# Edge payload in another space, a join that doesn't wait for it, and twenty chunks of own rows gathered in the sort phase

## The reference, cut to what matters

```python
# layer 0: softmax aggregation over the edges of a node, then an MLP 32 -> 64 -> 32
msg   = relu(h[src]) + 1e-7
alpha = segment_softmax(msg * beta, dst)
out   = mlp(segment_sum(msg * alpha, dst) + h)
# layer 1: an MLP on [h_dst, h_src - h_dst] of each edge, with two batch norms
# layer 2: two spline convolutions over the 3 attributes of an edge
# layer 3: three convolutions (GINE) over the 8 attributes of an edge
```

## Time and profile before

| | us |
|---|---|
| median of 3 timed runs | 6416.72 |
| their range | 6408.68 to 6420.33 |
| span of the profiled execution | 7419.8 |
| VectorE busy, GpSimd busy | 4474.0, 4471.1 |
| end of the sort phase in the profile | about 1349 |
| end of layer 0 in the profile | about 1995 |

### The profile page before, as it was taken

One profiled execution on the slowest core, in us unless ns is written; L12 is line 12 of the kernel. 1 busy time (PEld: TensorE's weight loads), 2 busy tenths in 40 slices (PEclk: granted clock), 3 DMA queues, 4 the chain that ended last, 5 costly groups with the idle time before them and its releaser, 6 DMA issues. The chain is left out here.

```text
span 7419.8 us, 40111 instructions
## 1 busy us (share of the span) xinstructions
PE 2391.5 (32%) x7897; PEld 1532.4 (21%) x7897; DVE 4474.0 (60%) x8498; ACT 1488.7 (20%) x2709; POOL 4471.1 (60%) x4334
## 2 busy tenths in 40 slices
PE   0000000001422220003556577623336665666222
PEld 0000000000311110001334355422223332333111
DVE  8745978896278583545888567646645554555111
ACT  0000000120201120101212122234424443444000
POOL 7777571577367527755553466467756646563666
PEclk9999999998655565555666677755568887887555
DMA  1111110111277511312322122255534433443111
GB/s 41 30 37 16 34 26 4 24 23 22 61 100 112 81 44 40 79 51 58 71 67 60 31 53 53 43 76 90 93 54 70 70 64 58 69 70 65 41 43 36
DMA packets 646154, 400.37 MB, mean 54 GB/s; under 512 B 357903, under 2 KB 603572, under 8 KB 645671
## 3 DMA queue, kind: packets, MB, share of 16 engines
q0 software_dynamic: 138304, 79.39, 14.4%
q1 hardware_dynamic: 488316, 291.24, 13.7%
q10 hardware_dynamic: 19306, 27.35, 1.1%
HBM read 221.09 MB, written 179.22 MB: 54 GB/s over the span
## 5 line engine op out<-in xcount | busy, mean ns | idle before, releaser
L969 POOL DMA_INDIRECT gin_ring<-tab,QB x784 | 790.0, 1008 | 482.2 <-DVEq L2642 241.4
L969 POOL DMA_INDIRECT c_ring<-tab,QB x784 | 775.7, 989 | 432.0 <-issue 223.5
L1747 PE MATMUL c_psU<-spline,c_hzT 97*128 97x288 f32 x1568 | 633.6, 561 | 218.4 <-DVE c_V L1702 188.5
L969 POOL DMA_INDIRECT c_ring<-a_tab,b_place x392 | 383.7, 979 | 345.1 <-DMA x_lin<-c_ring 151.2
L1509 POOL DMA_INDIRECT nodes<-H,a_out x392 | 435.5, 1111 | 192.4 <-issue 127.0
L969 POOL DMA_INDIRECT l_ring<-in_x_dram,a_own x376 | 429.3, 1142 | 188.8 <-issue 114.3
L969 POOL DMA_INDIRECT sort_ring<-xe_tab,b_place x392 | 422.7, 1078 | 171.1 <-issue 118.9
L2692 POOL DMA_INDIRECT out_dram<-out_rowr,out_idxr x392 | 385.9, 984 | 203.4 <-issue 121.8
L969 POOL DMA_INDIRECT l_ring<-agg_tab,QA x392 | 404.6, 1032 | 156.3 <-issue 125.7
L969 POOL DMA_INDIRECT sort_ring<-in_x_dram,sort_raw x392 | 413.0, 1054 | 120.3 <-issue 119.2
L1747 PEld LDWEIGHTS c_psU<-spline,c_hzT 97*128 97x128 f32 x1568 | 390.8, 266 | 381.3 <-issue 259.7
(11 more groups left out here) (643 smaller groups left out, 7541.7 us busy)
## 6 DMA issues: line engine op xcount, KB each, us to landing
tab<-c_rows SPq DMA_DIRECT2D x147, 128.0 KB
a_tab<-l1s_rows SPq DMA_DIRECT2D x49, 304.0 KB
x_lin<-c_ring SPq DMA_DIRECT2D x49, 256.0 KB
c_din<-dst_lin SPq DMA_DIRECT2D x98, 128.0 KB
c_ring<-tab SPq DMA_DIRECT2D x98, 128.0 KB
c_ring<-tab,QB POOLq DMA_INDIRECT x784
dst_lin<-c_yd SPq DMA_DIRECT2D x98, 128.0 KB
c_xin<-x_lin SPq DMA_DIRECT2D x98, 128.0 KB
```

Of the source, the lines that this page charges most:

```text
L969: pool.indirect_dma_start(out=ring[:, at + j, :], out_offset=None, in_=table, in_offset=bass.IndirectOffsetOnAxis(ap=idx[:, w:w + 1], axis ...
L1747: ins = pe.matmul(self.psU[i % 2][:, t, 0:288], self.hzT[c % 2][:, (2 * i + t) * P:(2 * i + t + 1) * P], w[:, :, :].rearrange("p o j -> p ...
```

## The change

- `raw3` and `raw8` lie in the space of `rows_b` instead of that of `H`. The join no longer waits for `paid`; ScalarE waits for it ahead of the first `place`.
- `flag_segments` for the source order, and `flagged`, follow the join directly, ahead of the rank sort; the destination order's flags stay where both were.
- ScalarE places all 25 pairs ahead of the first square root, and between them waits for `ranked` and sends the ranks through DRAM, which SyncE did before.
- `PRE` is 20 instead of 2: 160 gathers of own rows stand in the sort phase, through a ring of four tiles (`NO`), and 29 chunks (232 gathers) are left to layer 0.
- SyncE reloads `PB` at pair 8 instead of pair 21.

```diff
-    copied_first = 21
-    copied_after = {8: range(21, 22), 9: range(22, 24), 10: range(24, pairs)}
+    NO, turned_back = 4, 8
...
-        own = [ph.sb(f"own{i}", [P, CH, D]) for i in range(g.PRE)]
+        own = [ph.sb(f"own{i}", [P, CH, D]) for i in range(NO)]
...
-        raw3, raw8 = (space[:, o * W:(o + n) * W].rearrange("p (w c) -> p w c", c=n) for o, n in ((0, 3), (3, 8)))
+        early = rows_b[:, :, :].rearrange("p w f -> p (w f)")
+        raw3, raw8 = (early[:, o * W:(o + n) * W].rearrange("p (w c) -> p w c", c=n) for o, n in ((0, 3), (3, 8)))
...
             for q in range(pairs):
-                if q == copied_first:
+                if q == turned_back:
                     sp.wait_ge(pkept, 16)
                     sp.dma_start(PB[:, :], g.pb_lin.rearrange("(p w) -> p w", w=W)).then_inc(pback, 16)
-                    sp.wait_ge(ranked, 1)
-                    sp.dma_start(g.qa_lin.rearrange("(p f) -> p f", f=SF), net.CW[0][0:SR, 0:Q4, :].rearrange("p q r -> p (q r)").bitcast(I32)).then_inc(qkept, 16)
...
-            sp.wait_ge(qkept, 16)
-            sp.dma_start(QA[:, :], g.qa_lin.rearrange("(p w) -> p w", w=W)).then_inc(qback, 16)
             for c in range(g.PRE):
-                sp.wait_ge(owngot[c], 16 * CH)
-                sp.dma_start(lin(g, g.xs_lin, c), own[c][:, :, :]).then_inc(ownkept, 16)
+                sp.wait_ge(owngot[c % NO], 16 * CH * (c // NO + 1))
+                sp.dma_start(lin(g, g.xs_lin, c), own[c % NO][:, :, :]).then_inc(ownkept[c % NO], 16)
...
             pool.wait_ge(flagged, 1)
             for c in range(g.PRE):
-                gather_from(g, pool, a["x"], A.own, own[c], c, 0, owngot[c])
+                if c >= NO:
+                    pool.wait_ge(ownkept[c % NO], 16 * (c // NO))
+                gather_from(g, pool, a["x"], A.own, own[c % NO], c, 0, owngot[c % NO])
...
+            act.wait_ge(paid, 2 * pairs)
...
-            for q in range(copied_first):
+            for q in range(pairs):
                 if q == free:
                     act.wait_ge(joined, 1)
                 place(q)
+            act.wait_ge(ranked, 1)
+            act.dma_start(g.qa_lin.rearrange("(p f) -> p f", f=SF), net.CW[0][0:SR, 0:Q4, :].rearrange("p q r -> p (q r)").bitcast(I32)).then_inc(qkept, 16)
+            act.wait_ge(qkept, 16)
+            act.dma_start(QA[:, :], g.qa_lin.rearrange("(p w) -> p w", w=W)).then_inc(qback, 16)
             for q, cs in enumerate(groups):
                 norm_act(g, act, act_in, act_out, q + 1, len(cs) * CH, t[q % 2])
-                for p in copied_after.get(q, ()):
-                    place(p)
...
-            v.memset(space[:, 0:11 * W], 0.0).then_inc(blank, 1)
+            v.memset(early[:, 0:11 * W], 0.0).then_inc(blank, 1)
...
-            v.wait_ge(paid, 2 * pairs)
             join.forward(v, link, keyf, slot)
             join.match(v, link)
             join.back(v, link)
             v.sem_inc(joined, 1)
+            v.wait_ge(back, 16 * 3)
+            flag_segments(g, v, link, K[0], A, before[0], after[0], edged, 16 * 4)
+            v.sem_inc(flagged, 1)
...
             v.sem_inc(ranked, 1)
             weights.finish(v, filled)
-            v.wait_ge(back, 16 * 3)
-            for i, F in enumerate((A, B)):
-                flag_segments(g, v, link, K[i], F, before[i], after[i], edged, 16 * 4)
-            v.sem_inc(flagged, 1)
+            flag_segments(g, v, link, K[1], B, before[1], after[1], edged, 16 * 4)
...
-    g.PRE, g.DELTA = 2, N + CH
+    g.PRE, g.DELTA = 20, N + CH
```

More of the change, by code:

```diff
@@ L625, in order_edges @@
     wide = D + g.CB - 1
-    copied_first = 21
-    copied_after = {8: range(21, 22), 9: range(22, 24), 10: range(24, pairs)}
+    NO, turned_back = 4, 8
     S0 = 112
     FULL, REST = g.FULL, g.REST
-    assert copied_after[10].stop == 25 and len(groups) == 13
+    assert len(groups) == 13
     with Phase(g, "sort") as ph:
@@ L637, in order_edges @@
         hgot, hcopied = [ph.sem(f"hgot{i}") for i in range(NE)], ph.sem("hcopied")
-        flagged, owngot, ownkept = ph.sem("flagged"), [ph.sem(f"owngot{i}") for i in range(g.PRE)], ph.sem("ownkept")
+        flagged, owngot, ownkept = ph.sem("flagged"), [ph.sem(f"owngot{i}") for i in range(NO)], [ph.sem(f"ownkept{i}") for i in range(NO)]
         akept = [ph.sem(f"akept{i}") for i in range(2)]
@@ L708, in _ @@
                 sp.dma_start(lin_pair(g, g.xd_lin, q), H[:, of_pair(q), :]).then_inc(akept[q % 2], 16)
-            sp.wait_ge(qkept, 16)
-            sp.dma_start(QA[:, :], g.qa_lin.rearrange("(p w) -> p w", w=W)).then_inc(qback, 16)
             for c in range(g.PRE):
-                sp.wait_ge(owngot[c], 16 * CH)
-                sp.dma_start(lin(g, g.xs_lin, c), own[c][:, :, :]).then_inc(ownkept, 16)
+                sp.wait_ge(owngot[c % NO], 16 * CH * (c // NO + 1))
+                sp.dma_start(lin(g, g.xs_lin, c), own[c % NO][:, :, :]).then_inc(ownkept[c % NO], 16)
             for i in range(2):
                 sp.wait_ge(akept[i], 16 * ((pairs + 1 - i) // 2))
-            sp.wait_ge(ownkept, 16 * g.PRE)
-            sp.wait_ge(qback, 16)
+            for i in range(NO):
+                sp.wait_ge(ownkept[i], 16 * ((g.PRE + NO - 1 - i) // NO))
             sp.wait_ge(pback, 16)
@@ L784, in _ @@
                 place(q)
+            act.wait_ge(ranked, 1)
+            act.dma_start(g.qa_lin.rearrange("(p f) -> p f", f=SF), net.CW[0][0:SR, 0:Q4, :].rearrange("p q r -> p (q r)").bitcast(I32)).then_inc(qkept, 16)
+            act.wait_ge(qkept, 16)
+            act.dma_start(QA[:, :], g.qa_lin.rearrange("(p w) -> p w", w=W)).then_inc(qback, 16)
             for q, cs in enumerate(groups):
                 norm_act(g, act, act_in, act_out, q + 1, len(cs) * CH, t[q % 2])
-                for p in copied_after.get(q, ()):
-                    place(p)
+            act.wait_ge(qback, 16)
         @block.vector
```

## The result

| | before | changed |
|---|---|---|
| median of four runs each, us | 6418.52 | 6537.24 |
| range, us | 6408.68 to 6423.67 | 6527.14 to 6537.66 |
| ratio, with its 95% interval | | 1.0175 [1.0164, 1.0187] |

The change costs 118.7 us. The forecast had the sign and the mechanism, and too little of it: +78, 6495. The ratio puts the kernel at 6529 from the median that the forecast started from (6416.72), inside the range of 6385 to 6535; the median itself, 6537, lies 2 us above the range's upper end.

The account below looks back on a forecast made before the run. The prediction took VectorE to bound layer 0 in either kernel and GpSimd to end the changed sort phase: +78 there (1263 − 1185), 0 in layer 0, so 6416.72 + 78 = 6495; range 6385 to 6535, its own 6440 to 6530.

Parts of the forecast that it names:

- The slow beat: Sort phase and layer 0: VectorE's slow stretches beside gathers, read as the cost of recording and left out of the sum.
- e: Part of each gather's own beat that belongs to recording; taken as 0.05 us, with 0 to 0.22 kept for the range.
- Two thirds: Sort and layer 0: 231 of the 354 us in which their gathers wait vanish at e = 0; guided e = 0.05.
- the 991: Seven later stretches: 991 us by which they would shrink if GpSimd never waited.
- the prediction's own equation: Record's excess over the timed runs: 1003 = 231 + 991 f at e = 0, giving f = 0.78.
- its list: Change in time by e: 0 gives +96, 0.05 +79, 0.1 +52, 0.15 +24, 0.2 −3, 0.25 −25, 0.305 −8.
- The join's wait: Sort phase: join no longer waits for payload copies and runs 361 to 583, 86 us sooner than in the rebuilt kernel.
- the placing: Sort phase: norm queued behind the last placed pair, runs 1064 to 1159; VectorE waits some 60 us ahead of it.
- the prediction's second sign of being wrong: Layer 0 in the timed run bound by GpSimd, so that taking 144 gathers out of it pays.
- Rival 1: The beat of the gathers is recording, e of 0.2 or more; some −20, 6395; chance 0.14.
- rivals 2 and 3: Rival 2: first record holds as it stands, 6300, chance 0.08; rival 3: slow beat belongs to the chip, 6440, chance 0.07.
- Rival 4: Both paths come out even, e of 0.17 to 0.2; 6417, chance 0.11.

Follow-up runs that it names:

- second record: The kernel before, unchanged, recorded once more; span 6418.3 us, one run's median 6420.12 us.
- nine records: Records of the kernel before (its second), the changed kernel and seven variants of the two; medians from 6368.35 to 6571.74 us.
- early join alone: Kernel before with raw payload in the edge-row table's space and no wait ahead of the join; 6368.35 us, ratio 0.9921.

## Why the prediction was right in its sign and short in its size

**The slow beat (left out of the sum rightly, shown).** That VectorE's slow beat is in no timed run is shown by the second record of the kernel before and by that of the changed one; that recording made it stays argued. The forecast that the changed kernel's record would again span 7400 to 7500 was wrong: the beat did not return in any of nine records.

**The term that was mis-sized: e, and the gathers' prices with it.** "Two thirds lies between the first two, so I take e = 0.05." The gather's beat has no part that belongs to recording: in the changed kernel's record, as long as the timed runs, 41 gathers from 1000 to 1050 us, with VectorE idle, read as in the earlier trace rows, and the first gather of the kernel before reads in its second record as in the earlier trace rows:

```profile
L971 POOL DMA_INDIRECT sort_ring<-xe_tab,b_place x41 | 38.7, 944 | 12.5 <-issue 12.5
...
L969 POOL DMA_INDIRECT sort_ring<-in_x_dram,sort_raw x392 | 412.9, 1053 | 120.4 <-issue 119.2 <-DMA sort_raw<-in_dst_dram 1.2
```

0.944 + 0.305 = 1.25 us, so e = 0. The estimate carried the share that sort and layer 0 lose, two thirds, over to the later stages, which no row of the first record could settle. By the second record the later stages shrank by 762 us (5424.6 to 4662.5), 0.77 of the 991, and the prediction's own equation asks for 0.78 at e = 0. At e = 0 its list says +96, of which layer 0 gives 10 back. The rest of the difference stands in the terms:

| term, us | forecast at e = 0.05 | measured |
|---|---|---|
| keys decoded | 361 | 346 |
| join, rank sort | 222, 409 | 208, 406 |
| sort phase before ends | 1185 | 1190 |
| first gather beside the join ends | 526 | 558 |
| second gather of the changed kernel ends | 1056 | 1091 |
| 160 own gathers end | 1258 | 1306 |
| sort phase of the changed kernel ends | 1263 | 1314 |
| layer 0, before and changed | 554, 554 | 566, 553 |

The keys were 15 us sooner because the forecast took the slow beat out of the stretch from 302 us on only: by 302 us VectorE had done 397 instructions in the first record and 415 in the second. That made the kernel before no faster, only VectorE's wait for the copies longer. That its sort phase ends nearly where it was forecast (1190 against 1185) is luck: the join began 19 us later than the forecast had it (466 against 447, most of it e) and took 14 us less.

On the changed side the phase ended 51 us later than forecast, and 32 of these stood there when the first gather was done: 392 at 1.41 us beside VectorE instead of 1.33. Of these 32, 20 are e, and 12 come from pricing gathers beside the join as those beside the key sort. The second gather was only 3 us longer than forecast, since the ranks came 31 us sooner (965 against 996) and more of it ran with VectorE idle: luck again. The own rows took 215 us instead of 202, 8 of it e. Windows of the changed kernel, columns as in the earlier trace rows, beside the norm and after it:

```profile
1096.00:1182.00 86.00, 0.00 (x0) 0.00 (x0) 80.74 (x94) 4.74 (x14) 68.63 (x58) 1.00 0.12 24
1182.00:1306.00 124.00, 0.00 (x0) 0.00 (x0) 0.00 (x0) 0.00 (x0) 93.85 (x100) 1.00 0.13 26
```

By these windows a gather took 1.48 us beside the norm, where the prediction priced it like those beside the key sort (1.38, or 1.33 less e); with VectorE idle it took 1.24. In sum the sort phase grew by 124 instead of 78, and layer 0 gave 13 back instead of nothing; 111 of the 118.7 us. The other 8 lie in the spread of the later phases.

**The change part by part.** The join's wait, the flags and the placing went as forecast in kind: the wait gone, the flags 3.6 us earlier in the queue, the norm held behind the last pair, no wait in the ring of four. VectorE stood idle 113 us ahead of the norm, not 60. That layer 0 gives nothing back held for all but the first 13 us; to that extent the prediction's second sign of being wrong, a layer 0 bound by GpSimd, was there.

**The rivals.** Rival 1 needed e of 0.2, rivals 2 and 3 the slow beat in the timed runs; the second record takes all three away. Rival 4 falls with rival 1. What none of them had is what the experiments found: 53 us to be won with the early join and the own gathers left where they were.

## What to carry to other kernels

A bound has to be looked up for each phase: moving work of one engine from one phase into another pays only while that engine sets the end of the phase that the work leaves, and it is free only while that engine stands idle at the end of the phase that it enters. In the kernel before GpSimd set layer 0's end by 13 us and stood idle for 74.54 us at the end of the sort phase, so about a chunk more there (8 gathers at 1.45 us in layer 0) would have won nearly all of the 13 us for nothing; this is an estimate that no run tests. With the join early GpSimd sets the end of the sort phase too, and from 8 chunks on each gather moved cost its full 1.23 us. Where a record is much longer than the timed runs, take a second one before anything is rebuilt from the first: the share e, which only the rebuilding needed, made 18 of the 41 us that the forecast lacks (+96 at e = 0, +78 forecast).

## What the runs showed of the hardware that was not expected

One engine's work can be stretched in a record while another engine's beside it is not: in the first record VectorE did one instruction for each gather in 224 us (161 and 161), in the second 292 beside 153, and the spans were 7419.8 and 6418.3 us. No run shows what did that. A gather's busy time on GpSimd goes with what VectorE does: 0.944 us with VectorE idle, and beside the norm 1.222 us (33 own gathers from 1100 to 1150 us of the changed kernel) and 1.213 us (51 table gathers from 1030 to 1106 us of the early join alone), so that hiding the norm behind the gather gave back 15.6 us of what it hid. The first of these groups (count, busy us, mean ns, idle before):

```profile
L971 POOL DMA_INDIRECT sort_own<-in_x_dram,a_own x33 | 40.3, 1222 | 10.1 <-issue 10.1
```

and the second of these groups:

```profile
L970 POOL DMA_INDIRECT sort_ring<-xe_tab,b_place x51 | 61.9, 1213 | 15.5 <-issue 15.5
```
